# Half of the weight loads of two set-up stages on ACT's DMA queue, and four slots for the output weights

## The reference

```python
mod = (_silu(c) @ wmod).reshape(2, 6, 1, -1)       # wmod is 512 x 3072
sa, ca, ga, sb, cb, gb = (mod[:, i] for i in range(6))
ga = (2 * (ga >= 0) - 1) * jnp.maximum(jnp.abs(ga), 0.25)   # gb likewise
h = _layernorm(x) * (1 + ca) + sa
x = x + ga * attention(h)
h = _layernorm(x) * (1 + cb) + sb
x = x + gb * feed_forward(h)
```

## Time and profile before

| | |
|---|---|
| median of 3 runs | 2636.64 us (2635.79 to 2637.99) |
| time of the profiled execution | 2633.9 us |
| span of its trace | 2632.0 us |
| PE busy | 2154.1 us (82%) |
| DVE / ACT / POOL busy | 1197.0 / 873.5 / 397.9 us |
| DMA, mean of the span | 71 GB/s |
| `modulation` of layer 0, first DMA to last result | 4.4 to 48.9 us |
| `join_weights`, first DMA issue to last store landed | 50.4 to 117.3 us |
| `modulation` of layer 1 | 1622.9 to 1667.3 us |

### The profile page before, as it was taken

The page is one execution under the profiler, slowest core; times in us unless marked ns, Lnnn a source line. Parts: engine busy times, 40 slices in busy tenths (PEclk is TensorE's granted clock), DMA queues, the critical chain, the costliest instruction groups (busy, mean ns, idle before and its releaser), DMA issues. The chain is left out here.

```text
span 2632.0 us, 33740 instructions
## 1 busy us (share of the span) xinstructions
PE 2154.1 (82%) x12048; PEld 1229.2 (47%) x12048; DVE 1197.0 (45%) x3459; ACT 873.5 (33%) x1566; POOL 397.9 (15%) x309
## 2 busy tenths in 40 slices
PE   6444899999999999999958686476699999999678
PEld 4142455555555555556624343344344444443233
DVE  2043655544444454445114234122567776775145
ACT  0032233433333333344401011022055555565211
POOL 0001133333333333333300000000000000000000
PEclk7567699999999999999979898576679998998789
DMA  4522222222222222222050403122412222210221
GB/s 161 183 77 54 52 52 69 69 69 69 69 69 69 69 69 69 69 69 66 26 181 16 172 8 120 60 101 97 75 29 43 43 43 43 43 27 19 85 93 39
DMA packets 96346, 186.71 MB, mean 71 GB/s; under 512 B 26443, under 2 KB 33483, under 8 KB 95987
## 3 DMA queue, kind: packets, MB, share of 16 engines
q1 hardware_dynamic: 96178, 184.56, 26.5%
HBM read 97.45 MB, written 30.93 MB: 49 GB/s over the span
## 5 line engine op out<-in xcount | busy, mean ns | idle before, releaser
L710 ACT ACTIVATE at_prob<-at_scp 128x512 f32<-128x512 f32 (+1 forms) x608 | 350.0, 576 | 599.7 <-PE at_scp L813 589.3
L1385 ACT ACTIVATE as_prob<-as_scp 128x1024 f32<-128x1024 f32 (+3 forms) x384 | 306.7, 811 | 230.5 <-PE as_scp L1476 172.4
L744 DVE CUSTOM_DVE_ANT_0 at_junk<-at_mxp,causal 128x128 f32<-128x128 f32 (+3 forms) x512 | 242.1, 486 | 232.3 <-PE at_mxp L822 219.2
L1488 PE MATMUL as_mxp<-l_keys,as_q 48*128 48x512 f32 (+2 forms) x768 | 295.8, 478 | 58.6 <-DVE as_mxf L1432 20.2
L822 PE MATMUL at_mxp<-l_khi,at_qhi 96*128 96x512 f32 (+2 forms) x768 | 304.9, 438 | 34.0 <-DVE at_tm L768 16.7
L1437 DVE CUSTOM_DVE_ANT_0 as_junk<-as_mxp,causal 128x384 f32<-128x384 f32 (+3 forms) x512 | 228.2, 488 | 97.1 <-PE as_mxp L1488 94.3
L809 PE MATMUL at_scp<-at_qhi,l_khi 97*128 97x512 f32 (+1 forms) x608 | 246.0, 405 | 2.7 <-DMA at_qhi<-at_mrow 2.6
L655 POOL TENSOR_TENSOR at_pre<-at_prob 128x512 f32<-128x512 f32 x128 | 160.5, 1285 | 518.5 <-ACT at_prob L710 507.2
L812 PE MATMUL at_scp<-at_qlo,l_khi 96*128 96x512 f32 (+1 forms) x608 | 235.5, 387 | 0.0
L1488 PEld LDWEIGHTS as_mxp<-l_keys,as_q 48*128 48x128 f32 x768 | 131.1, 199 | 223.5 <-DVE as_mxf L1432 82.8
L813 PE MATMUL at_scp<-at_qhi,l_klo 96*128 96x512 f32 (+1 forms) x608 | 233.9, 385 | 0.0
(11 more groups left out here) (198 smaller groups left out, 2658.2 us busy)
## 6 DMA issues: line engine op xcount, KB each, us to landing
at_qhi<-at_shi SPq DMA_DIRECT2D x192, 128.0 KB, 2.4
at_qlo<-at_slo SPq DMA_DIRECT2D x192, 128.0 KB, 2.4
m_w<-in_wmod SPq DMA_DIRECT2D x12, 1024.0 KB, 10.7
jw_wo<-in_wo_t SPq DMA_DIRECT2D x8, 1024.0 KB, 8.2
at_spread<-l_recips SPq DMA_DIRECT2D x64, 128.0 KB, 2.7
l_o<-at_u_sb SPq DMA_DIRECT2D x16, 512.0 KB, 3.4
as_q<-scratch_queries SPq DMA_DIRECT2D x48, 128.0 KB, 4.9
as_q<-l_queries_b SPq DMA_DIRECT2D x48, 128.0 KB, 4.4
```

The costliest lines, as they stand in the source:

```text
L710: nc.scalar.activation(prob[:, x % RING0, c0:HALF], scp[x % BANKS0][:, c0:HALF], ACT.Exp).then_inc(s["exp_done"], 1)
L744: nc.vector.tensor_tensor_reduce(out=junk[:, u % 2, 0:w], in0=tile[:, 0:w], in1=k.causal[:, HALF - w:HALF], scale=1.0, scalar=LOWEST, op0= ...
L1385: nc.scalar.activation(prob[:, r:r + 2, c0:HALF], scp[p % 2][:, :, c0:HALF], ACT.Exp).then_inc(s["exp_done"], 1)
L1488: nc.tensor.matmul(mxp[banks["max", u][0]][:, 0:w], q[t % SLOTS1][rows, j // 2, qt * P:(qt + 1) * P], k.keys[rows, t // NG, k0:k0 + w], st ...
```

## The change

The parts of the modulation matrix go to SP's and ACT's queues in turn: SP issues parts 2, 0 and 3, ACT issues parts 5, 1 and 4 ahead of its exponential. In `join_weights` the groups get four slots in place of two. SP loads the even groups, ACT the odd ones: 1 and 3 at once, and 5 and 7 between its wait for PE's group `g` (1 and 3) and its copy of that group. SP loads groups 0 and 2 without a wait, then the stores of groups 0 and 1, load 4, stores 2 and 3, load 6, stores 4 and 5, and stores 6 and 7. Amounts of data and computation are the same.

```diff
@@ modulation @@
             def _(sp):
                 sp.dma_start(cin[:], c_t).then_inc(s["c_in"], 16)
-                for part, arrived in ((GATE[0], "gate_a_in"), (GATE[1], "gate_b_in"), *((part, "cols_in") for part in KIND)):
+                for part, arrived in ((GATE[0], "gate_a_in"), *((part, "cols_in") for part in KIND[0::2])):
                     sp.dma_start(w[:, :, part * D:(part + 1) * D],
                                  wmod[:, part * D:(part + 1) * D].rearrange("(k p) n -> p k n", p=P)).then_inc(s[arrived], 16)
             @block.scalar
             def _(act):
+                for part, arrived in ((GATE[1], "gate_b_in"), *((part, "cols_in") for part in KIND[1::2])):
+                    act.dma_start(w[:, :, part * D:(part + 1) * D],
+                                  wmod[:, part * D:(part + 1) * D].rearrange("(k p) n -> p k n", p=P)).then_inc(s[arrived], 16)
                 act.wait_ge(s["c_in"], 16)
@@ join_weights @@
-        wo = sb("wo", [VD, 2, G, D])
+        WO = 4
+        wo = sb("wo", [VD, WO, G, D])
...
-                for g in range(NG):
-                    if g >= 2:
-                        sp.wait_ge(s["vo_psum"], g - 1)
-                    sp.dma_start(wo[:, g % 2, :, :], t["wo_t"][g * G:(g + 1) * G].rearrange("h p n -> p h n")).then_inc(wo_in[g % 2], 16)
+                for g in range(0, NG, 2):
+                    if g >= WO:
+                        sp.wait_ge(s["vo_psum"], g - WO + 1)
+                    sp.dma_start(wo[:, g % WO, :, :], t["wo_t"][g * G:(g + 1) * G].rearrange("h p n -> p h n")).then_inc(wo_in[g % WO], 16)
                     if g >= 2:
                         store(g - 2)
+                        store(g - 1)
...
                 for g in range(NG):
-                    pe.wait_ge(wo_in[g % 2], 16 * (g // 2 + 1))
+                    pe.wait_ge(wo_in[g % WO], 16 * (g // WO + 1))
...
             @block.scalar
             def _(act):
+                def odd(g):
+                    act.dma_start(wo[:, g % WO, :, :], t["wo_t"][g * G:(g + 1) * G].rearrange("h p n -> p h n")).then_inc(wo_in[g % WO], 16)
+                for g in range(1, WO, 2):
+                    odd(g)
                 for g in range(NG):
                     act.wait_ge(s["vo_psum"], g + 1)
+                    if g % 2 == 1 and g + WO < NG:
+                        odd(g + WO)
                     if g >= 2:
                         act.wait_ge(vo_out[g % 2], 16 * (g // 2))
                     nc.scalar.activation(vo[:, g % 2, :], vps[:, g % 2, :], ACT.Copy).then_inc(s["vo_done"], 1)
```

More of the change, by code:

```diff
@@ L171, in join_weights @@
         sb = lambda n, s, d=F32: ctx.enter_context(nc.sbuf_tensor("jw_" + n, s, d))
-        s = semaphores(ctx, nc, "jw_", "small_in wo_in0 wo_in1 lat_psum lat_done rope_done wq_out vo_psum vo_done vo_out0 vo_out1")
-        wo_in, vo_out = (s["wo_in0"], s["wo_in1"]), (s["vo_out0"], s["vo_out1"])
+        s = semaphores(ctx, nc, "jw_", "small_in wo_in0 wo_in1 wo_in2 wo_in3 lat_psum lat_done rope_done wq_out vo_psum vo_done vo_out0 vo_out1")
+        WO = 4
+        wo_in, vo_out = [s[f"wo_in{i}"] for i in range(WO)], (s["vo_out0"], s["vo_out1"])
         nope = sb("nope", [NOPE, H, QA])
@@ L219, in _ @@
                     for j in range(G):
-                        mm = nc.tensor.matmul(vps[LAT * j:LAT * (j + 1), g % 2, :], wv[:, g * G + j, :], wo[:, g % 2, j, :],
+                        mm = nc.tensor.matmul(vps[LAT * j:LAT * (j + 1), g % 2, :], wv[:, g * G + j, :], wo[:, g % WO, j, :],
                                               start=True, stop=True)
```

## The result

The changed kernel took 2647.03 us (median of 11 runs, 2640.92 to 2663.44) against 2636.64 us: a ratio of 1.0046, with a 95% interval of 1.0024 to 1.0068, which is 6 to 18 us. It is 0.46% slower, clear of zero, and outside the predicted range. Measured once more (experiment 12) it was 1.0053 (1.0028 to 1.0078).

What follows compares the result with a forecast made beforehand. Bounds: the first gate part's landing in modulation; small arrays, then DMA-limited loads in `join_weights`. Terms 4.4 + 2.7 - 8.0 = -0.9 us took 2636.6 to 2635.7 us, range 2629.5 to 2641.5 us.

Steps and rivals of the forecast that it cites:

- What bounds the stages: Modulation: PE waits for the first gate part's landing; `join_weights`: small arrays, then group loads, DMA-limited to within 10%.
- three signs of being wrong: ACT issues over 1.5 us, first gate part landing as early as before, or group 4 not waiting for load 4.
- Modulation: Matrix on two queues: first gate part delayed 2.2 us in each of two layers, 4.4 us lost in all.
- the table load: Modulation: ACT's 1.28 us activation table load, if ahead of its issues, starts them 0.9 us behind SP's; delay 1.8 us.
- The working of `rep`: Modulation: `rep` ready at 9.5 us behind ACT's three issues, covered by the gate part landing at 12.4 us.
- Small arrays: `join_weights`: ACT's loads of groups 1 and 3 beside the small arrays delay these by 2.7 us (0 to 5.4).
- The 67.5 us of this paragraph: `join_weights`, small arrays: time after which another 2.1 MB take 5.4 us, so all seven transfers are in by T0.
- Groups: `join_weights`: from group 0's start T0, last copy ends at T0 + 26.3 us, saving 8.0 us (6.8 to 10.4).
- a second queue can't give much; the earlier start can: `join_weights` groups: engines work 9.2 us per pair against periods of 10.47 and 10.04 us; four slots use the idle stretch.
- That the first transfers aren't slowed: Rival, modulation and small arrays: issues already in the engines finish first; -5.3 to -8.0 us, faster; chance 0.20.
- The stores did get late: Rival, `join_weights`: stores behind loads 4 and 6 delay copies; 5.3 us saved, +1.8 in all, no change; chance 0.12.
- The rival on the other side: ACT held at its own issues in modulations and groups; slower by 5.3 us from 2.0 us an issue; chance 0.10.

Runs made afterwards that it cites:

- experiment 12: The changed kernel itself measured once more, against the kernel before: 1.0053 (1.0028 to 1.0078), +14 us (7 to 20).
- experiment 1: Only the modulation part of the change (matrix parts on SP's and ACT's queues), `join_weights` as before; against the kernel before: 1.0054 (1.0036 to 1.0071), +14 us.
- experiment 8: Kernel before with the first gate part third of SP's six issues, ACT's queue unused; against before: 1.0041 (1.0018 to 1.0064), +11 us.
- experiment 4: Modulation part alone with gate parts swapped: ACT issues part 2, SP part 5; `join_weights` as before; against before: 1.0021 (1.0001 to 1.0041), +5.5 us.
- experiment 5: Modulation part alone, but ACT issues its three parts behind its exponential; `join_weights` as before; against before: 1.0014 (0.9992 to 1.0036), no measurable difference.
- 2: Only the `join_weights` part of the change, modulation as before; against the kernel before: 0.9990 (0.9975 to 1.0005), no measurable difference.
- experiment 3: Modulation as before; `join_weights` with four slots, every load and store on SP's queue; against before: 0.9957 (0.9944 to 0.9969), -11 us.
- 6: Modulation split with ACT issuing behind its exponential and a wait for the first gate part; `join_weights` as before; against before: 1.0013 (0.9986 to 1.0039).
- experiment 7: Modulation as before; `join_weights` as changed, but ACT issues groups 1 and 3 only after the small arrays landed; against before: 0.9952 (0.9925 to 0.9980).
- experiment 11: Modulation as before; four slots, all loads on SP's queue, ACT issuing each store behind its copy; against before: 0.9973 (0.9957 to 0.9989), -7 us.

## Why the prediction was wrong

**What bounds the stages** was read rightly: PE's wait for the first gate part, the small arrays and then the loads. Experiments 1 and 8 show it: what the gate part loses, the stage loses, layer by layer. None of the three signs of being wrong that it named came: ACT's issues were short, the gate part was late, and group 4 waited for load 4. They watched for other errors than the one that was made.

**Modulation: the step that failed.** The prediction put the delay at 2.2 us a layer, between nothing and "2.7 us, if ACT's part 5 starts together with it and takes half of the rate". It was 4.63 and 4.77 us. The equal share was right, and is the 2.7 us. What I had left out, and so put at nothing, is that the second queue to be issued to doesn't start beside the first: its data come 2 us later. I had treated an equal share from the first byte as the worst case, and in the table load I had looked only for reasons why ACT's queue might be the later one. The table load went behind ACT's three issues (6.02 us), so ACT was first by 0.43 us, and that decided it: in experiments 4 and 5 the first gate part is on the queue that is issued to first, and PE starts at 9.83 and 10.30 us. The working of `rep` was right, 9.5 us against 9.37 us measured, though it counts the exponential's 0.21 us twice (8.16 - 6.11 = 2.05 us has it already).

**Small arrays: the same step.** Predicted 2.7 us (0 to 5.4), measured 5.7 us. The turns by packets were right (22 packets of the one beside 23 of the other), with about 2.4 us of late start on top: SP's first data 3.7 us behind its issue in place of 1.3 us. The remaining 0.6 us isn't accounted for. The rule of the modulation fits less well here. SP and ACT issue within 0.01 us of each other, and ACT's data were first in all three traces (after, 2 and 12). SP's came 3.7, 2.9 and 3.3 us behind the issue, when ACT's queue had moved 0.69, 0.42 and 0.52 MB, and not its whole first transfer of 1.05 MB. Why ACT's queue is first at such a tie, no run shows. The 67.5 us of this paragraph of the prediction follows from nothing in it, and nothing in the sum uses it.

**Groups.** Predicted 8.0 us saved, measured 9.8 (11.8 and 11.3 in experiments 12 and 2). The sum came out near, but its course was not the forecast one: group 4 started at T0 + 15.4 us in place of 12.8, behind a wait of 9.6 us in place of about 5, since load 4 shared the engines with load 5 all the way, and group 6 at T0 + 20.2 us in place of 22.0. The granted clock didn't stay at 0.50, as said above. The premise that "a second queue can't give much; the earlier start can" was right and went too little far: experiment 3 shows that the second queue takes away 0.8 to 3 us here (21.7 us against 22.5 to 24.6 us), and 2.8 us where PE's last groups ran at the same clock.

**The rivals.** That the first transfers aren't slowed is refuted for the kernel as changed, though it holds for whichever queue is first. ACT was not held at its issues (0.44 to 0.53 us each in the modulations). The stores did get late (copy 3 waited 4.84 us for one), but under the wait for load 4, as that rival's sum had it. The rival on the other side named the wrong mechanism, so its 0.10 was no cover: the slower result was given 0.11.

**The sum.** With the terms as measured it is 4.7 + 4.9 + 5.7 - 9.8 = +5.5 us, and +5.8 us by the stages. The measured +12 us (6 to 18) and +14 us (7 to 20) are more. Part of it is the granted clock of TensorE. In three sets of runs of before its mean over the span was 0.8798, 0.8795 and 0.8814, in the two sets of the changed kernel 0.8781 and 0.8777. A straight line through each set of runs (time over mean clock) puts the changed kernel at 2645.9 us for a clock of 0.880 (both sets together), and before at 2637.9 us: +8 us. The other 4 to 6 us go with the lower clock. The same done with each experiment and its own set of before gives +11 and +8 us for experiments 1 and 8, where the stages lost 9.7 and 11.1 us, and -2 to 0 us for 4, 5 and 6. So at equal clock the time follows the gate part to within about 3 us; a line through six to twelve runs is rough. Whether the change lowers the clock or chance did is open: experiments 4, 5 and 6, whose gate part is on time, had 0.876 to 0.877 as well, 2, 3, 7 and 11, with the modulation of before, 0.881 to 0.883, but experiment 8, which uses no second queue at all, 0.878, like experiment 1. Experiment 11's -7 us beside a stage 13.7 us shorter, and experiment 7's -13 us beside 9.5 us, show that single kernels scatter by that much in this program. I don't claim more than +5.8 us for the mechanism.

## What to carry to other kernels

A second DMA queue gave nothing here, where one already fills the engines (388 GB/s), and it took the order away: what was needed first had to be issued first, on whichever queue, and the rest only behind it. Ask of each split of loads which transfer is on the critical path, which queue is issued to first, to the tenth of a microsecond, and how large that one's first transfer is. The gain in this change was the two extra slots, which use an idle stretch of the DMA engines; with them on one queue the kernel is 0.43% faster than before (0.31% to 0.56%). What comes behind the last group, 11 us with the store of `wq` in it, is the next place to look: experiment 11 has 7.5 us there.

## What the runs showed of the hardware

- In the modulations the queue issued to second starts when the other has moved about its first transfer: with 1 MB ahead its data come 4 us behind the issue (0.43 us of lead are enough, and it goes either way), with 256 KB ahead about 2 us behind it, where alone the first packets took 1.1 us and the full rate 2.2 us. In `join_weights`, with both issued at once, SP's data come 2.9 to 3.7 us behind in place of 1.3 us, after 0.4 to 0.7 MB of ACT's.
- While both queues have data to move they move equal numbers of packets (192 and 190 in 2 us), not bytes: 0.36 MB in 16 KB packets beside 0.05 MB in 2 KB packets in the same 2 us.
- A modulation whose gate part is on time took 46 us or 49 us: 45.8 to 46.3 us in seven of these stages over all traces, 48.8 to 49.5 us in nine, both kinds with the code of before. In experiment 3's layer 0 (49.5 us) the gate products took 16.98 us in place of 15.81 us, and the two-column products 24.66 us in place of 22.62 us. In the latter the granted clock fell from 1.00 (2.4 GHz) to 0.50 (1.2 GHz) after fewer products, as these windows of before and of experiment 3 show (columns as in the earlier trace rows); the 1.2 us of the gate products it doesn't show:

```profile
30.00:32.00 2.00, 2.00 (x16) 2.00 (x15) 0.00 (x0) 0.00 (x0) 0.00 (x0) 0.75 0.03 8
```
```profile
26.00:28.00 2.00, 2.00 (x11) 1.26 (x10) 1.74 (x3) 0.00 (x0) 0.00 (x0) 1.00 0.00 0
...
30.00:32.00 2.00, 2.00 (x13) 2.00 (x12) 0.69 (x1) 0.00 (x0) 0.00 (x0) 0.55 0.00 0
```

- The attention of layer 1, the same code in all traces, took 608.6 to 637.9 us, with a mean granted clock of 0.88 to 0.81: a spread larger than anything that this change moved.
